# Gated messages: the destination rows are added in a TensorE bank and ScalarE copies the sum out

## The reference, cut to what matters

```python
h = jnp.maximum(_layernorm(x, axis=-1), 0.0)
x_t = _mlp2(h, W1n, b1n, W2n, b2n)                # leaky_relu between two matmuls
e_t = _mlp2(edge_attr, W1e, b1e, W2e, b2e)
msgs = x_t[src] * e_t * dp_scale
aggregated = jax.ops.segment_sum(msgs, dst, num_segments=num_nodes)
out = h + aggregated * res_w
mu, var = ...
x = x + (out - mu) * jax.lax.rsqrt(var + EPS) * gamma + beta
```

## Time and profile before

| what | value |
|---|---|
| median of 3 runs | 5541.77 us |
| profiled execution | 5537.43 us, its span 5535.3 us |
| PE (TensorE matmul) | 64% of the span, 15275 instructions |
| DVE (VectorE) | 73%, 6567 instructions |
| ACT (ScalarE) | 50%, 6379 instructions |
| POOL (GpSimd) | 66%, 3647 instructions |
| mean granted TensorE clock | 0.780 of full speed |

### The profile page before, as it was taken

How to read it: one execution, slowest core, us unless ns; L and a number is a source line. 1 busy time by engine, 2 the same in 40 slices (tenths; PEclk the granted TensorE clock), 3 DMA queues, 4 the chain that set the end, 5 groups by cost and what they waited for, 6 DMA issues and landing times. The chain is left out here.

```text
span 5535.3 us, 72269 instructions
## 1 busy us (share of the span) xinstructions
PE 3564.5 (64%) x15275; PEld 1835.2 (33%) x15275; DVE 4044.6 (73%) x6567; ACT 2757.9 (50%) x6379; POOL 3627.5 (66%) x3647
## 2 busy tenths in 40 slices
PE   8992788847776999677728867777455545661110
PEld 5551555523332333244414433333222212221000
DVE  8873698857774555699869969999555569996442
ACT  6662677733331222476629966666322247772221
POOL 7777277757775777577713347665377767765777
PEclk9996999978785555699959989999666668885555
DMA  8549977754442222466514433333344423322221
GB/s 99 74 62 43 109 232 232 230 146 108 103 108 55 62 62 62 134 212 195 183 60 138 135 98 84 84 84 84 91 129 132 125 68 77 77 68 67 70 74 48
DMA packets 535690, 595.56 MB, mean 108 GB/s; under 512 B 297571, under 2 KB 312041, under 8 KB 533948
## 3 DMA queue, kind: packets, MB, share of 16 engines
q1 hardware_dynamic: 319036, 473.91, 29.2%
q0 software_dynamic: 112896, 91.81, 9.2%
q10 hardware_dynamic: 103648, 28.71, 6.6%
HBM read 354.69 MB, written 303.31 MB: 119 GB/s over the span
## 5 line engine op out<-in xcount | busy, mean ns | idle before, releaser
L1165 POOL DMA_INDIRECT l_got<-d_x,l_near x1176 | 1139.2, 969 | 562.1 <-issue 373.7
L1173 POOL DMA_INDIRECT ln_xd<-d_xt,idsE x392 | 370.1, 944 | 208.3 <-issue 119.2
L2480 POOL DMA_INDIRECT out<-fi_res,fi_near x392 | 381.1, 972 | 181.0 <-issue 118.5
L1165 POOL DMA_INDIRECT p_got<-d_sums,p_near x392 | 399.5, 1019 | 151.7 <-issue 150.5
L948 POOL DMA_INDIRECT d_pos<-placeE,finE x392 | 401.9, 1025 | 146.4 <-issue 135.6
L1165 POOL DMA_INDIRECT p_got<-d_h,p_near x392 | 384.8, 982 | 156.5 <-issue 117.2
L1165 POOL DMA_INDIRECT p_got<-d_ext,p_near x392 | 378.5, 965 | 162.8 <-issue 117.1
L892 PE MATMUL ps<-hot_lo,hot_w 128*128 128x392 bf16 x2352 | 391.9, 330 | 15.6 <-ACT hot_w L930 15.6
L930 ACT ACTIVATE hot_w<-hot_hi,vals 128x128 bf16<-128x128 bf16 x784 | 267.9, 393 | 126.2 <-DVE hot_lo L787 114.5
L411 PE MATMUL ps<-ident,fi_sums 64*128 64x64 f32 x392 | 53.1, 314 | 424.8 <-DVE fi_sums L1338 424.8
L1338 DVE TENSOR_TENSOR_SCAN p_sums<-same,p_sums,ps 65x1024 f32<-65x1024 f32 (+1 forms) x98 | 229.5, 2342 | 95.1 <-PE ps L1437 90.9
(11 more groups left out here) (388 smaller groups left out, 10934.3 us busy)
## 6 DMA issues: line engine op xcount, KB each, us to landing
l_xd<-d_x SPq DMA_DIRECT2D x147, 256.0 KB
d_ext<-ln_ext SPq DMA_DIRECT2D x98, 264.0 KB, 2.2
d_xt<-in_x_wide ACTq DMA_DIRECT2D x49, 520.0 KB
ln_x<-in_x SPq DMA_DIRECT2D x98, 256.0 KB
d_h<-ln_hb SPq DMA_DIRECT2D x98, 256.0 KB, 3.0
d_x<-ln_x SPq DMA_DIRECT2D x98, 256.0 KB
lb_x<-d_x SPq DMA_DIRECT2D x49, 512.0 KB
d_x<-lb_x SPq DMA_DIRECT2D x49, 512.0 KB
```

The costliest lines, as they stand in the source:

```text
L1165: nc.gpsimd.indirect_dma_start(out=out[:, q], out_offset=None, in_=source, in_offset=bass.IndirectOffsetOnAxis(ap=ids[:, q:q + 1], axis=0) ...
L1173: nc.gpsimd.indirect_dma_start(out=out[:, q], out_offset=None, in_=source, in_offset=bass.IndirectOffsetOnAxis(ap=ids[:, g, q:q + 1], axis ...
L2480: nc.gpsimd.indirect_dma_start(out=out, out_offset=bass.IndirectOffsetOnAxis(ap=near[:, r, q:q + 1], axis=0), in_=res[:, r, q], in_offset= ...
```

## The change

The sum `l_xd` + bank 6 leaves VectorE. `rows_by` gets one more matmul, with the identity as weights and the destination rows as the 512 moving columns, that adds them into bank 6 before the four gamma matmuls; ahead of it TensorE waits for the load of the rows. ScalarE then copies bank 6 into `l_x`, at tick 8. `l_o` is now made one turn earlier for its group, at the end of the turn (tick 13) and ahead of `l_d_rstd`, which goes to tick 14, as does `l_hd`. On ScalarE `l_hid` goes from tick 7 to tick 5.

```diff
-def rows_by(nc, out, paired, weights, W):
+def rows_by(nc, out, paired, weights, W, rows=None):
     nc.tensor.matmul(out, W.ones_split[:], W.beta_split[:], start=True, stop=False)
+    if rows is not None:
+        nc.tensor.matmul(out, W.ident[:], rows.rearrange("p s c -> p (s c)"), start=False, stop=False)
...
@block.vector
                 def dests(i, r, g):
-                    yield from norm_d.dve(nc, dve, g, r, xd[:, r], ticks=(7, 8, 11, 12, 13))
+                    yield from norm_d.dve(nc, dve, g, r, xd[:, r], ticks=(7, 8, 11, 12, 14))
                 def outputs(i, r, g):
+                    yield 13
                     dve.wait_ge(norm_d.scaled, g + 1)
                     dve.wait_ge(m["back"], g + 1)
                     nc.vector.scalar_tensor_tensor(out=o1[:], in0=as_rows(bank(1)), scalar=col["res"], in1=hd[:, r % 2],
                                                    op0=ALU.mult, op1=ALU.add).then_inc(m["o1_done"], 1)
+
+                def normed(i, r, g):
                     yield 1
...
-                def result(i, r, g):
-                    yield 10
-                    dve.wait_ge(st[r % 2], half_turns(i, r) * 16 + 16)
-                    dve.wait_ge(m["residual"], g + 1)
-                    nc.vector.tensor_tensor(x2[:, r % 2], xd[:, r], as_rows(bank(6)), ALU.add
-                                            ).then_inc(m["x2_done"], 1)
-                ring_loop(dve, GROUPS, [sources], [], [sums_of, dests], [], [outputs], [result])
+                ring_loop(dve, GROUPS, [sources], [], [sums_of, dests], [outputs], [normed])
@block.tensor
                     hold(pe, m["xf_done"], g + 1)
                     hold(pe, m["x2_done"], g + RING)
-                    rows_by(nc, bank(6), xf[:], W.gamma1, W).then_inc(m["residual"], 1)
+                    hold(pe, x_in[r], i * 16 + 16)
+                    rows_by(nc, bank(6), xf[:], W.gamma1, W, xd[:, r]).then_inc(m["residual"], 1)
@block.scalar
                     nc.scalar.activation(hf[:], bank(0), ACT.Copy).then_inc(m["hf_done"], 1)
-                    yield 7
+                    yield 5
                     act.wait_ge(m["mm1"], g + 1)
...
                 def dests(i, r, g):
-                    ... ticks=(8, 12, 13), kept=1)
+                    ... ticks=(8, 12, 14), kept=1)
...
                     nc.scalar.activation(xf[:], bank(7), ACT.Copy).then_inc(m["xf_done"], 1)
+                    yield 8
+                    act.wait_ge(st[r % 2], half_turns(i, r) * 16 + 16)
+                    act.wait_ge(m["residual"], g + 1)
+                    nc.scalar.activation(x2[:, r % 2], as_rows(bank(6)), ACT.Copy).then_inc(m["x2_done"], 1)
```

More of the change, by code:

```diff
@@ L2187, in dests, with normed @@
                 def dests(i, r, g):
-                    yield from norm_d.act(nc, act, g, r, hd[:, r % 2], ACT.Relu, m["o1_done"], ticks=(8, 12, 13), kept=1)
-                def outputs(i, r, g):
+                    yield from norm_d.act(nc, act, g, r, hd[:, r % 2], ACT.Relu, m["o1_done"], ticks=(8, 12, 14), kept=1)
+                def normed(i, r, g):
                     yield from norm_o.act(nc, act, g, 0, ticks=(2, 6))
@@ L2196, in residual @@
                     nc.scalar.activation(xf[:], bank(7), ACT.Copy).then_inc(m["xf_done"], 1)
-                ring_loop(act, GROUPS, [sources], [b], [dests], [], [outputs], [residual])
+                    yield 8
+                    act.wait_ge(st[r % 2], half_turns(i, r) * 16 + 16)
+                    act.wait_ge(m["residual"], g + 1)
+                    nc.scalar.activation(x2[:, r % 2], as_rows(bank(6)), ACT.Copy).then_inc(m["x2_done"], 1)
+                ring_loop(act, GROUPS, [sources], [b], [dests], [], [normed], [residual])
 def relu_messages(nc, A, sem, W, D, bank, out):
```

## The result

| | before | changed |
|---|---|---|
| median of 20 runs each, same chip | 5542.22 us | 5553.19 us |
| ratio, 95% interval | | 1.0022, 1.0014 to 1.0029 |
| span of the profiled execution | 5535.3 us | 5549.5 us |
| mean of a full turn | 12.46 us | 12.70 us |
| VectorE instructions in a full turn | 20 | 19 |

The kernel became 0.22% slower, 11 us by the medians, at the bound of what the prediction called measurable. 5555 us was forecast, within 5530 to 5571. A full turn is measured from one `l_s_sum` to the next, over the 43 such steps between turns 5 and 48: 535.81 us before (3351.30 to 3887.11), 545.87 us now (3355.08 to 3900.95). That is 0.23 us a turn, 10 us over 44 turns, so the loss lies in the full turns and little is left for ramp and drain.

What follows compares the result with a forecast made beforehand. The prediction took a loop through VectorE and ScalarE to bound the kernel. Per turn, -0.64 + 0.52 + 0.42 = +0.30 us over 44 turns, +13 us on 5541.77, gave 5555 us, range 5530 to 5571.

Steps and rivals of the forecast that it cites:

- The loop: From one `l_s_sum` to the next through VectorE and ScalarE: seven steps, 12.35 us before, set the turn.
- The addition leaving VectorE: Beside `l_hn`, ahead of a 0.40 us wait: removing its 0.60 us is worth nothing, `l_d_rstd` only waits longer.
- `l_o` off the loop: Between `l_d_rstd` and the next `l_s_sum`: its 0.64 us moves into the wait, worth -0.64 a turn.
- The copy on the loop: On ScalarE between `l_d_sq` and `l_hn`: adds 0.52 us a turn, ends 0.50 and 0.60.
- The turn at full clock: The new loop through VectorE and ScalarE: 12.23 us, 0.12 less than before.
- The new matmul hidden at full clock: On TensorE between beta and gamma, 0.88 us: gamma ends at 8.49, the copy can't start before 9.46.
- The clock: Stretches at 1.2 GHz delay TensorE's work ahead of ScalarE's copy: +0.42 us a turn, ends 0 and 0.73.
- The sum: Over 44 full turns: -0.64 + 0.52 + 0.42 = +0.30 us each, +13 us in all.
- Everything else: TensorE's wait for loaded rows, SyncE's issues behind `l_x`, ramp and drain: nothing, 3 us either way for the range.
- Rival 1: Slow stretches fall on message matmuls with 1.10 us to spare, or become rarer: 5537 us, chance 0.26.
- rival 2: VectorE sets the pace, so less work on it gains 26 to 44 us: 5516 down to 5498, chance 0.06.
- rival 3: TensorE's single idle time brings a slow stretch every turn, copy 0.73 late each time: 5569 us, chance 0.15.

Runs made afterwards that it cites:

- e1: Kernel before with only `l_o` moved to the end of the turn, ahead of `l_d_rstd`; the addition stays on VectorE: ratio 0.9963 to before, 11.94 us a turn.
- e2: Changed kernel with ScalarE's copy moved behind `l_d_sd` (tick 12 instead of 8): ratio 0.9943 to the kernel before, 11.79 us a turn.
- e4: Changed kernel with two unused matmuls in TensorE's idle time ahead of the `w1n` matmuls: ratio 0.9978 to the kernel before, 12.20 us a turn.
- e9: Changed kernel with `l_o` back at the start of the turn and two unused matmuls in TensorE's idle time: ratio 1.004 to before, 12.91 us a turn.
- e8: Kernel before with two unused matmuls in TensorE's idle time: ratio 1.001 to the kernel before, 12.42 us a turn.
- e5: Changed kernel with the copy behind `l_d_sd` and two unused matmuls in TensorE's idle time: ratio 0.994 to the kernel before, 11.72 us a turn.
- e3: Changed kernel without the matmul that adds the destination rows, so the output lacks them: ratio 0.9988 to the kernel before, 12.36 us a turn.
- e6: Changed kernel with `l_o` back at the start of the turn, behind `l_d_rstd`: ratio 1.0086 to the kernel before, 13.52 us a turn.
- e7: Changed kernel with `l_hid` back behind the two roots on ScalarE (tick 7): ratio 1.0021 to the kernel before, 12.66 us a turn.

## Why the prediction was right, point by point

- **The loop bounds the kernel, not VectorE.** Right. The changed kernel does less on VectorE and is slower; e1 does as much as before and is faster. The Trainium skill's page "Perfetto Trace Analysis" (Identifying the Most-Contended Engine) points to the engine of the highest occupancy, and by that rule the change was a gain. The runs disagree for the kernel before, whose VectorE was 94% busy. Once the loop is broken, as in e1, VectorE no longer waits and sets the pace; that less work on it then helps shows only in e2, which has the addition off VectorE too and takes 0.15 us a turn less than e1, not 0.60.
- **The addition leaving VectorE: 0.** Right. `l_d_rstd`'s wait took it over: 0.81 at full clock (e4), where 0.8 was forecast. No run takes the addition away alone, but e9 less e8, both filled and with `l_o` on the loop, is 12.91 - 12.42 = 0.48 us (from 12.905 and 12.423); that is the price of the copy by itself, and nothing is left for the addition.
- **`l_o` off the loop: -0.64.** Right: 0.70 between e9 and e4, at full clock. Against the kernel before alone it shows as 0.52 (e1), since VectorE then becomes the bound.
- **The copy on the loop: +0.52.** 0.48, both from start to start in e4 and from e4 less e5, a little below the lower end of 0.50.
- **The turn at full clock: 12.23 without the branch.** 12.14 in e4's turn. Besides the copy, `l_d_xc` to `l_d_sq` took 0.73 in place of 0.79.
- **The new matmul hidden at full clock, 0.97 us to spare.** Right: in e4's turn gamma ends at 3615.11 and the copy starts at 3616.15, 1.04 later, without a wait.
- **The clock: +0.42, ends 0 and 0.73.** It cost 0.49. In the 43 full turns 31 stretches begin in the changed kernel, 0.72 a turn, and 28 in the kernel before, the 0.65 of the forecast; so they became somewhat more frequent, as allowed for. The late turn above has the copy 0.79 late, where 0.73 was forecast for a full stretch. But the forecast path carries only part of the 0.49: against e4, the step from `l_d_sq` to the copy is 0.38 longer in the mean of the full turns (0.91 after 0.54). Another 0.10 lies ahead of it, between `l_d_xc` and `l_d_sq` (0.83 after 0.73): a late `l_hid` holds up the roots and `l_d_sq`, as in e3. The prediction had counted `l_hid` at full clock alone and has no term for this, so that its total came as near as it did is in part luck. e3 shows that the new matmul's length is what uses up the copy's spare time: without it the turn is 0.33 shorter at no better clock.
- **The sum: +0.30 a turn.** +0.23. By means of full turns, the part at full clock is -0.26 (e4 less before), where -0.12 was forecast, and the clock's +0.49, where +0.42 was: two small misses that partly cancel. Of the first, 0.09 is the shorter steps above; the kernel before pays at least 0.04 for its own low clock (by e8, which lifts it to 0.95), which the forecast had at nothing and a gain at full clock includes.
- **Everything else: nothing.** Nearly: `l_s_rstd` waits 4.7 us in 500, 0.12 a turn, for ScalarE's root behind a late `l_hid`. It was not forecast; in e4 it is absent, so it is the clock's, the sign of the 0.10 above.

Rival 1 (the clock holds where it matters) is out by the late turns, rival 2 (VectorE sets the pace) by the 43.6 us of waits, and rival 3 (a stretch in every turn) by the 31 stretches in 43 turns. Rival 1 is what e4 makes of the kernel, and rival 2 is close to what e2 makes of it.

By the Trainium skill's page "TensorE: Matmul & The Clock Gate" (What's actually happening), the slow clock is the default and activity releases it; e4 agrees, where two more matmuls a turn in the idle time (1.98 us busy) took the clock from 0.90 to 1.00. In the changed kernel, 0.88 us more at a place that was busy already raised nothing (0.91 to 0.90).

What stays open: ramp and drain were not measured alone; in which turns the clock falls, and for how long, was read from the traces but not explained.

## What to carry to other kernels

Look for the wait that comes back every turn, and follow it around: an engine that is 94% busy can be inside a loop that another engine closes; here taking 0.60 us of work a turn off it was worth nothing, while the place of one instruction in that loop was worth 0.5 to 0.9 us. Work moved to an idle engine must also not stand on the loop there: moved behind the root, the same copy turned a loss of 0.22% into a gain of 0.57%. Where an engine's slack is what hides stretches of low clock, added work is to be counted at the low clock, not at the full one, and on every path that starts behind it: here the late `l_hid` was the one that the prediction missed.

## What was not expected of the hardware

- More work made the kernel faster: two unused matmuls, 1.98 us busy a turn, in TensorE's idle time held its clock at 1.00 and took the changed kernel from 12.70 to 12.20 us a turn (e4). In the kernel before the same two took the clock only from 0.91 to 0.95 and gained nothing (e8).
- Stretches of low clock came in two lengths, 3.4 us and 6.8 us. In their full turns the kernel before and the changed one show only 3.4 (28 and 31 of them); of e6's 24, 17 last 6.8 us, of e3's 31 two, of e7's 28 one. What decides between the two was not tried.
- Idle time of the same 2.04 us was followed by a fall of the clock in one turn of the changed kernel and by none in the next; idle times of 2.83 to 2.87 us went with a stretch of low clock in all 13 turns that have them.
